# Flamingo block with two expert layers: plain scatters in layer 0, separate first groups, and weighted sums with the values as a 32-wide stationary operand

## The reference

```
x = x + tanh(g_xattn[0]) * attention0(layernorm(x), ctx)          # 16 heads of 16, biases, output projection
x = x + tanh(g_ffn[0])   * experts0(layernorm(x))                 # 8 experts, top 2, softmax gates, relu, F = 1024
x = x + tanh(g_xattn[1]) * attention1(layernorm(x), ctx, mask)    # 16 heads, causal, no output projection
x = x + tanh(g_ffn[1])   * experts1(layernorm(x))                 # 8 experts, sparsemixer top 2, silu(gate) * up, F = 512
```

## Time and profile before

| | |
|---|---|
| median of 3 runs | 1835.96 us (1834.67 to 1841.45) |
| the profiled execution | 1848.75 us, its span 1845.8 us |
| TensorE (PE) busy | 1653.4 us |
| VectorE (DVE), ScalarE (ACT), POOL busy | 1246.7, 1235.0, 876.2 us |
| share of the chain that ended last: TensorE, VectorE, ScalarE, DMA | 62%, 13%, 7%, 5% |

### The profile page before, as it was taken

One profiled execution on the slowest core, in us unless ns is written; L12 is line 12 of the kernel. 1 busy time (PEld: TensorE's weight loads), 2 busy tenths in 40 slices (PEclk: granted clock), 3 DMA queues, 4 the chain that ended last, 5 costly groups with the idle time before them and its releaser, 6 DMA issues.

```text
span 1845.8 us, 36500 instructions
## 1 busy us (share of the span) xinstructions
PE 1653.4 (90%) x12444; PEld 1559.8 (85%) x12444; DVE 1246.7 (68%) x2829; ACT 1235.0 (67%) x2873; POOL 876.2 (47%) x877
## 2 busy tenths in 40 slices
PE   3999989999499999999988599999999299999997
PEld 2898888888398988999988499989998299999997
DVE  2566656555578888898886456666666767676764
ACT  1666666656288877887876276666666177777775
POOL 2123332232456656676665311333332457777776
PEclk8999999999599999999999799999999599999999
DMA  2222221213567877888874322323322378888883
GB/s 94 47 58 75 66 67 47 75 53 92 147 185 211 220 204 204 219 223 211 213 201 129 91 53 63 85 83 87 87 58 81 117 205 232 232 232 230 228 232 108
DMA packets 215785, 255.90 MB, mean 139 GB/s; under 512 B 30768, under 2 KB 166192, under 8 KB 215472
## 3 DMA queue, kind: packets, MB, share of 16 engines
q1 hardware_dynamic: 185360, 218.26, 41.4%
q0 software_dynamic: 28608, 33.73, 9.3%
q10 hardware_dynamic: 1632, 1.59, 0.3%
HBM read 190.38 MB, written 49.97 MB: 130 GB/s over the span
## 4 chain that ended last, share of the span: by engine, by line
PE 62%; DVE 13%; ACT 7%; issue 6%; DMA 5%; POOL 2%; SPq 2%; another core or an unknown queue 2%; POOLq 0%; ACTq 0%; DVEq 0%
PE ps L372 13%; PE ps L374 13%; PE ps L373 13%; PE ps L490 11%; PE ps L392 5%; DVE KXR L1067 4%; DVE PTR L1096 3%; DMA U<-in_wpack 3%; DVE WR L1096 2%; ACT U L683 2%; PE ps L408 2%; PE ps L471 1%; ACT KXR L653 1%; POOL xs_scr L1175 1%
## 5 line engine op out<-in xcount | busy, mean ns | idle before, releaser
L1067 POOL TENSOR_TENSOR KXR<-U,KXR 128x1024 fp32r<-128x1024 f32 (+1 forms) x156 | 390.2, 2501 | 200.6 <-ACT KXR L653 200.6
L372 PE MATMUL ps<-QR,KXR 128*128 128x256 f32 x1248 | 363.4, 291 | 36.2 <-issue 23.2
L373 PE MATMUL ps<-QR,KXR 128*128 128x256 f32 x1248 | 356.1, 285 | 0.0
L374 PE MATMUL ps<-QR,KXR 128*128 128x256 f32 x1248 | 356.1, 285 | 0.0
L653 ACT ACTIVATE KXR<-U 128x1024 fp32r<-128x1024 f32 (+1 forms) x312 | 286.6, 945 | 78.3 <-DMA U<-in_wpack 55.7
L564 ACT ACTIVATE U<-ps,mx 128x128 f32<-128x128 f32 x1024 | 292.3, 381 | 13.0 <-DVE mx L927 7.5
L490 PE MATMUL ps<-VA,U 128*128 128x102 f32 x2048 | 271.1, 275 | 13.5 <-DVE U L937 9.5
L490 PEld LDWEIGHTS ps<-VA,U 128*128 128x128 f32 x2048 | 260.0, 194 | 25.3 <-DVE U L937 10.9
L372 PEld LDWEIGHTS ps<-QR,KXR 128*128 128x128 f32 x1248 | 240.0, 192 | 44.9 <-issue 29.3
L927 DVE TENSOR_REDUCE mx<-ps 128x4 f32<-128x512 f32 x256 | 175.4, 685 | 144.1 <-PE ps L408 62.0
L373 PEld LDWEIGHTS ps<-QR,KXR 128*128 128x128 f32 x1248 | 240.1, 192 | 0.0
(11 more groups left out here) (194 smaller groups left out, 4105.2 us busy)
## 6 DMA issues: line engine op xcount, KB each, us to landing
U<-in_wpack SPq DMA_DIRECT2D x234, 512.0 KB
U<-xs_scr SPq DMA_DIRECT2D x78, 258.0 KB
U<-in_wpack SPq DMA_DIRECT2D x78, 256.0 KB
KXR<-U SPq DMA_DIRECT2D x512, 32.0 KB
U<-in_ctx_t SPq DMA_DIRECT2D x16, 512.0 KB, 4.9
XR<-in_L_ffn_b SPq DMA_DIRECT2D x39, 128.0 KB
X<-in_x SPq DMA_DIRECT2D x8, 512.0 KB, 4.2
x_scr<-X SPq DMA_DIRECT2D x8, 512.0 KB
```

The costliest lines, as they stand in the source:

```text
L372: e.matmul(o, wh, xh, start=first, stop=False)
L373: e.matmul(o, wh, xl, start=False, stop=False)
L374: return e.matmul(o, wl, xh, start=False, stop=done)
L1067: e.tensor_tensor(w_cols(L, WL, n), w_raw(L, n), hi, ALU.subtract).then_inc(*l_w[n](L, i))
```

## The change

Three things are changed together.

Layer 0's experts write their rows, unscaled, to a place of their own for each of a token's two choices (`ys_scr`, 2 x 4096 rows), with a plain scatter. The gates stay in SBUF (`GT`), rows to the experts are one column shorter (`ROWS`), `act_y` is gone from layer 0, and so are the stores of `X`, which stays in SBUF. In layer 1 SP loads two rows per token (`sp_rows`) and VectorE adds both to `X`, multiplied by the gates (`dve_add_rows`).

The first group of each layer is written out apart (`pe_first`, `act_first`, `dve_first`, `sp_first`), `FIRST` is -8: keys and values come ahead of turns and queries, each constant is waited for where it is used, they are loaded in another order, four more banks are used, and in layer 0 twelve matmuls on a cleared tile go first (`WARM`). Layer 1's query, key and value weights and first contexts are loaded from tile 2 of layer 0's experts on (`sp_ahead`) and split at its end.

In the weighted sums the values of a head with the column of ones and what follows it (32 columns, `VA` is now flat) are the stationary operand, and the transposed probabilities move. The four heads of a step go to four groups of 32 partitions of `OB`. A batch's sums are copied out by ScalarE (`OS`), transposed by TensorE into a bank of `PTB`, which the probabilities' transposes share in turns (`pt_place`, `turn_free`), and then normalised; what follows comes one step later.

```diff
-                    for h in range(4):
-                        hh = 8 * m + 4 * z + h
-                        ins = e.matmul(OB[:, hh * 17:(hh + RV) * 17].rearrange("p (r d) -> p r d", r=RV), PT[:, i % 3, h],
-                                       VA[:, v, j % 2, hh:hh + 1, :].to_broadcast([128, RV, 17]), start=True, stop=True)
+                        w.wait_ge(*a_o[L, b - 1])
+                    for h in range(4):
+                        hh = 4 * (i % 4) + h
+                        ins = e.matmul(OB[32 * h:32 * h + 32, (i % 4) * 128:(i % 4) * 128 + 128], VA[:, v, j % 2, hh * 17:hh * 17 + 32],
+                                       PT[:, i % 3, h], start=True, stop=True)
...
+                if (b := bat(s, 6)) is not None:
+                    bank = pt_place["o", b]
+                    w.wait_ge(*a_o[L, b])
+                    turn_free(w, L, "o", b)
+                    for n in range(4):
+                        ins = e.transpose(bank[:, n * 128:(n + 1) * 128], OS[:, n * 128:(n + 1) * 128], ident)
+                    ins.then_inc(*m_o(L, b))
...
+                if (b := bat(s, 6)) is not None:
+                    w.wait_ge(*m_av[L, 4 * b + 3])
+                    if b:
+                        w.wait_ge(*m_o[L, b - 1])
+                    e.activation(OS[:, :], OB[:, :], ACT.Copy).then_inc(*a_o(L, b))
...
+        for n, (use, _, _) in enumerate(turns):
+            pt_place[use] = PTB[n % 2]
+            if n >= 2:
+                pt_before[use] = turns[n - 2][1:]
...
-                if (b := bat(s, 6)) is not None:
-                    w.wait_ge(*m_av[L, 4 * b + 3])
-                    o = OB[:, 0:272].rearrange("p (h d) -> p h d", d=17)
+                if (b := bat(s, 7)) is not None:
+                    w.wait_ge(*m_o[L, b])
+                    o = pt_place["o", b][:, :].rearrange("p (h d) -> p h d", d=32)
...
+        def pe_first(e, w, L):
+            if L == 0:
+                w.wait_ge(*s_kz[0, 0])
+                for n in range(WARM):
+                    e.matmul(PTB[1][:, :], KXR[:, 0:128], KXR[:, 0:512], start=True, stop=True)
+            for m in range(2):
+                pe_key(e, w, L, 0, m)
+            for h in range(2):
+                pe_value(e, w, L, 0, h)
+            for t in range(2):
+                pe_turn(e, w, L, 0, t)
+            for m in range(2):
+                w.wait_ge(*v_k[L, 0, m])
+                pe_query(e, w, L, 0, m)
...
+        def dve_add_rows(e, w, b):
+            w.wait_ge(*d_yl[b % 3][b])
+            e.scalar_tensor_tensor(X[:, b], YL[:, b % 3, 0], GT[:, 0, b:b + 1], X[:, b], ALU.mult, ALU.add).then_inc(*v_c.up())
+            w.wait_ge(*v_c.now)
+            e.scalar_tensor_tensor(X[:, b], YL[:, b % 3, 1], GT[:, 1, b:b + 1], X[:, b], ALU.mult, ALU.add).then_inc(*v_yl(b))
...
+                w.wait_ge(*v_h[0, NT - 1, 3])
+                sp_mask(e, w, 0)
                 experts_out(w, 0)
+                for b in range(3):
+                    sp_rows(e, w, b)
+                sp_keys(e, w, 1, 0)
+                sp_rows(e, w, 3)
+                sp_keys(e, w, 1, 1)
...
+        def sp_ahead(e):
+            for n, name in enumerate(("Wq", "Wk", "Wv")):
+                e.dma_start(WS[:, n], A["L1_xattn_" + name].rearrange("(t p) n -> p t n", p=128)).then_inc(*d_w2(n))
...
+                w.wait_ge(*m_y[L][L, i, a])
+                at = bass.IndirectOffsetOnAxis(ap=xi[:, i % 4, a:a + 1], axis=0)
+                if L == 0:
+                    ins = e.indirect_dma_start(ys_d[0], at, yo[:, r, a, :], None, bounds_check=2 * T - 1, oob_is_err=False)
+                else:
+                    ins = e.indirect_dma_start(ys_d[1], at, yo[:, r, a, :], None, bounds_check=T - 1, oob_is_err=False, compute_op=ALU.add)
```

More of the change, by code:

```diff
@@ L129, in grp @@
     g, m = divmod(s - k + 16, 16)
-    return g if m == 0 and 0 <= g < NG else None
+    return g if m == 0 and 0 < g < NG else None
 def bat(s, k):
@@ L346, in bank_free, with ct_low @@
                 w.wait_ge(*before[use])
+        def ct_low(L, g):
+            return (v_ct if (L, g) == (1, 0) else p_ct)[L, g]
         def banks_out(w, L):
@@ L520, in pe_down @@
             if i:
[L521 removed]
+                w.wait_ge(*m_y[L][L, i - 1, 1])
             for f in range(nf):
@@ new lines, in act_key @@
+        def act_key(e, w, L, g, m):
+            w.wait_ge(*m_k[L, g, m])
+            bank4 = place[L, "k", g, m][:, :].rearrange("p (b k) -> p b k", b=G)
+            if g >= 2 and m == 0:
+                for b in range((g - 1) * G - 2, (g - 1) * G):
+                    w.wait_ge(*d_k[b % 2][L, b, 7])
+            if L == 0:
+                w.wait_ge(*s_bq[0])
+                ins = e.activation(KT[:, g % 2, :, 0, m], bank4, ACT.Identity, bias=bqk[:, 1, m:m + 1])
+            else:
+                ins = e.activation(KT[:, g % 2, :, 0, m], bank4, ACT.Copy)
+            ins.then_inc(*a_k(L, g, m))
@@ L615, in act_attention @@
-                if L == 0 and (b := bat(s, 7)) is not None:
+                    act_context(e, w, L, g)
+                for at, take in ((X0, act_turn), (Q0, act_query), (K0, act_key), (V0, act_value)):
+                    for n in range(2):
+                        if (g := grp(s, at[n])) is not None:
+                            take(e, w, L, g, n)
+                if L == 0 and (b := bat(s, 8)) is not None:
                     w.wait_ge(*m_ot[b])
@@ new lines, in dve_key @@
+        def dve_key(e, w, L, g, m):
+            w.wait_ge(*a_k[L, g, m])
+            bank4 = place[L, "k", g, m][:, :].rearrange("p (b k) -> p b k", b=G)
+            hi, lo = KT[:, g % 2, :, 0, m].bitcast(F32), KT[:, g % 2, :, 1, m]
+            if L == 0:
+                ins = e.scalar_tensor_tensor(lo, bank4, bqk[:, 1, m:m + 1], hi, ALU.add, ALU.subtract)
+            else:
+                ins = e.tensor_tensor(lo, bank4, hi, ALU.subtract)
+            ins.then_inc(*v_k(L, g, m))
+        def dve_rests(e, w, L, s):
+            for at, rest in ((X0, dve_turn), (Q0, dve_query), (K0, dve_key)):
+                for n in range(2):
+                    if (g := grp(s, at[n])) is not None:
+                        rest(e, w, L, g, n)
+            if L == 0 and (b := bat(s, 8)) is not None:
@@ L1283, in sp_attention @@
+                if (b := bat(s, -8)) is not None and b >= 2:
+                    sp_keys(e, w, L, b)
                 if s == 121:
@@ L1305, in sp_experts @@
             for i in range(NT):
+                if L == 0 and i == 2:
+                    sp_ahead(e)
+                    for g in range(2):
+                        sp_context(e, w, 1, g)
                 if i + 2 < NT:
```

577 lines of the change are left out of this document (332 added, 245 removed).

## The result

The changed kernel takes 1758.3 us (median of 4 runs, 1754.96 to 1761.77), the kernel before 1836.45 beside it (1834.67 to 1841.45): a ratio of 0.957, with a 95% interval from 0.9542 to 0.9597. That is faster, by 78 us. The forecast was 1780 us with a range of 1720 to 1850. The profiled execution took 1754.96 us, its span 1753.2, against 1848.75 and 1845.8 before. So the two profiles lie 94 us apart, 16 more than the medians: the profiled execution of the kernel before was 12 us slower than its median.

What follows compares the result with a forecast made beforehand. TensorE was taken to bound attention, while something else held it up in layer 0's experts and at the starts. Terms -10 - 18 - 22 - 6 = -56 us gave 1793 profiled, 1780 on the median's basis; range 1720 to 1850.

Steps and rivals of the forecast that it cites:

- copy and transposes: Weighted sums: each batch adds a hidden ScalarE copy and four TensorE transposes, 0.36 us each batch, +23 us in all.
- the change of layers: Layer 1's start: weights fetched early, keys and values run while scatters land; first score earlier, -6 us (-12 to +3).
- the additions: Layer 1's attention: two more VectorE additions per batch, counted as hidden, 0 us (to +10).
- The likeliest case: Whole kernel: the eight sums' records partly overlap, held by instruction issue at 0.71 us a step; 1780 us, chance 0.42.
- The sums' matmuls: Attention's weighted sums: eight records a step fall from 0.87 to 0.71 us over 256 steps, -41 us (-72 to +18).
- I take 0.71, since nothing in the trace goes faster: Weighted sums: 16 instructions a step issue at 0.044 us each, as the transposes do, so a step takes 0.71 us.
- The five slots of the rival: Weighted sums: neighbouring heads overlap in program order, not held by issue; 0.59 us a step, -72 us, 1750 us; chance 0.27.
- the one given a chance of 0.04: Weighted sums: complete overlap of the heads in two slots, 0.24 us a step, -161 us, 1661 us; chance 0.04.
- the array empties: Weighted sums: each change of shape drains the array, 0.46 us more a step, 1.05 in all, +46 us, 1867; chance 0.18.
- the weighted sums together: Attention in both layers: matmuls -41, transposes +23, waits on the copy +5, later end of attention +3; -10 us in all.
- Plain scatters: Layer 0's experts: no scaling and shorter scatters on POOL free the next weights earlier; -18 us (0 to -35).
- First group of layer 0: Kernel start: keys and values come first, constants waited for where used; first score at 25.5 instead of 47.6, -22 us.

Runs made afterwards that it cites:

- a_oldsums: The changed kernel with the weighted sums of before (probabilities stationary, 102 value columns moving, no copy or transposes of sums): 1766.1 us, ratio 0.9757 to the kernel before.
- a_control2: The changed kernel unedited, run again in the third batch as the measure beside its edits: 1718.6 us, ratio 0.9495 to the kernel before.
- b_noscale: The kernel before without ScalarE's scaling by the gates in layer 0's experts, adding scatter kept: 1779.7 us, ratio 0.9846.
- b_plain: The kernel before with a plain scatter in layer 0, rows written over each other instead of added: 1777.9 us, ratio 0.9821.
- a_both: The changed kernel with layer 1's additions six steps earlier and the fourth batch's rows fetched ahead of the first key copies: 1712.7 us, ratio 0.9471.
- a_noadds: The changed kernel without layer 1's additions of expert rows except the first group's, rows still loaded: 1714.7 us, ratio 0.9471 to the kernel before.
- a_control: The changed kernel unedited, run in the second batch on a slower chip: 1762.7 us, ratio 0.9515 to the kernel before.

## Why the prediction came out as it did

The range held the time, and the sign was right; so were, nearly, the terms for copy and transposes, for the change of layers and for the additions. The likeliest case's account of the records was wrong. The 22 us between 1780 and 1758 look smaller than the errors in the terms: on the profiled executions, from which the terms were read, the forecast was 1793 and the time 1755.

**The sums' matmuls: forecast -41, by the rows -92 (256 x 0.36).** The step that failed is "I take 0.71, since nothing in the trace goes faster". The 16 instructions of a step start within 0.16 us, 0.010 each; the 0.044 read from the transposes was not the limit of the issue. The five slots of the rival were wrong too: 0.59 leaves no room for 0.36, and the records start in two rounds of four. Which head each belongs to, and so whether they leave the program's order, the trace does not tell. Two rivals were each half right. The overlap is complete, as in the one given a chance of 0.04: its two slots are 0.24 and measured 0.22. And a change of shape costs what stands between: 0.10 ahead, 0.05 behind and some 0.14 within, 0.29 a step against the 0.46 of "the array empties". By the rule that a change of tiling mode drains the engine (the Trainium skill, "TensorEngine Tiling (Array Packing)", Key Properties) the trace agrees that there is a price; whether it is a full drain no run here shows. Together 0.22 + 0.29 = 0.51, against the forecast 0.71. That the error stayed this small is luck: two things that the forecast held for rivals both happened, overlap worth (0.87 - 0.22) x 256 = 166 us and turns that cost 74.

**Of that gain a part came.** With +22 for the sums' transposes the rows make -70. a_oldsums against a_control2 shows what arrived, by their stages on chips that agree on the kernel before: layer 0's scores 375.9 to 344.3, layer 1's 374.3 to 347.0, -59; the two stretches behind the scores grew by 4.0 and 4.5, where +3 was forecast for both. In the median the ratios 0.9757 and 0.9495 differ by 0.026, 47 us, of which -10 had been forecast. So the weighted sums together, forecast -10, gave some -47 beside the other changes; this is the term that was furthest off. In the first comparison the attentions gave less, -28.5 and -4.2 with +2.0 behind them. There TensorE is idle for 23.8 us in layer 1's scores against 13.2 in a_control2; its waits in that stretch of the changed kernel show where:

```profile
PE ps L408 <- issue: 6.0, 8, 0.9
...
PE ps L469 <- issue: 2.2, 2, 1.7
```

The waits put down to "issue" are 10.0 us in all. The same kernel in a_control2 has none of them there; the last section has more on the chips.

**Copy and transposes: as forecast.** Four transposes of the sums take 0.35 to 0.36, 64 of them +23. The +5 for waits on the copy are hardly there: 1.0 us in layer 1's scores.

**Plain scatters: forecast -18 (0 to -35), measured -39.6, beyond the bound.** The mechanism stood: the plain scatter lasts 1115 ns on POOL instead of 1567, waits for nothing but the issue, and SP waits for the low half behind it for 58 us instead of 85 (560 to 900 us). Two sizes were off. TensorE's floor is 12.1 us a tile and not 11.7, and the tile reaches it, where I had left it 5% above and then taken half. b_noscale and b_plain show why half was wrong: either relief alone ends nearly all of TensorE's waits, so it was no matter of shares. The stage stands at TensorE's own time now, and nothing more is to be had there from POOL.

**First group of layer 0: forecast -22, measured -19.5 at the first score and -15.5 some steps on.** First score at 28.1 instead of 25.5. Two things were left out. The keys were counted at 0.235 a record: eight intervals at 0.43 instead add 8 x 0.19 = 1.5 us, over half of the 2.6. The twelve warming matmuls did not keep the clock up over the wait of 2.35 us; in a_control2 it fell within that wait, and all twelve key records came at 0.43. Whether they gave anything no run shows, for none leaves them out. And the forecast ended at the first score: the next group's context, now loaded behind the first group's inputs, holds up the fifth unit's scores by 3.5 us (5.2 to 5.4 in a_oldsums and a_control2), where the kernel before waits 0.7.

**Between the layers: forecast -6, measured -5.4.** The fourth batch's rows behind the key copies were the end of that chain, as the forecast said: a_both moves them, and 3.7 us more come off.

**Layer 1's additions: forecast 0 (to +10), measured 0 to +3.** a_noadds has 343.9 us of scores against 347.0, ratios 0.9471 against 0.9495 with intervals that overlap; in layer 0, where the two kernels do the same, their scores differ by 2.2. Beside the old sums they seem to cost more. Between b_plain and a_oldsums, both with the old sums, the scores grow by 5.5 us in layer 0 and 11.2 in layer 1. Of the 5.5, 4.5 are the wait ahead of the fifth unit's scores (5.2 us against 0.7). In layer 1 the largest part are waits of TensorE's sums for VectorE, which b_plain does not have; of a_oldsums:

```profile
PE ps L543 <- DVE U L1087: 6.8, 10, 0.9
```

L1087 is VectorE's product that normalises the sums of the batch before and frees their bank. With the new sums ScalarE's copy frees that bank, and of waits for the product only 2.3 us are left, in the transposes (a_control2). The forecast counted this at nothing, as mostly covered: so it was in b_plain, but not once the additions had come to VectorE. That the additions are the cause is argued and not shown: no run has the old sums without them.

## What to carry to other kernels

When a small stationary operand leaves most of TensorE's columns unused, put independent products in different groups of 32 output partitions: here their records overlapped fully. Then count the turns into and out of that shape, not the records: a turn cost 0.29 us here, more than the 0.22 of eight records, so gather all narrow work into as few turns as buffers allow. And when a stage has one engine ahead of all others, look for its floor first; here either of two reliefs gave nearly the whole distance, and the second added 0.1 to 0.3 us a tile. And when a start is brought forward, follow the chain some steps past the first result: the next load may be what is late.

## What the runs showed of the hardware

- Narrow products (128 rows, 32 columns, 128 moving f32 columns) take 0.11 us a record, and four groups of partitions run as fast as two. The 16 instructions of a step, loads and matmuls, start within 0.16 us.
- A turn from full-width matmuls into the 32-column form and back costs some 0.29 us in all: 0.10 ahead, behind transposes as behind scores, 0.14 within and at the end, 0.05 in the transposes behind.
- The same kernel took 1762.7 us on one chip and 1718.6 on another, and the kernel before 1851.5 and 1809.2: 44 and 42 us, with nearly the same ratio (0.9515 and 0.9495). The scores differ by 31.5 and 19.0 us (375.8 and 366.0 against 344.3 and 347.0), the stretches behind them by -3.7 and -2.8; the experts agree (473.1 and 472.4). On the slower chip TensorE's waits in layer 0's scores (30 to 340 us) name "issue", time in which it waited for nothing that the profile shows, and on the faster one they don't. a_control:

```profile
PE ps L408 <- issue: 9.2, 5, 4.0
```

  a_control2:

```profile
PE ps L408 <- ACT U L695: 6.0, 2, 5.4
```

  Those five waits are 9 of the 31 us of difference in that stage. The clock is about as much again: it falls in such waits or behind them, and stands at 0.50 in layer 0's scores for 27.3 us against 6.8; 20 us more at 0.43 a record instead of 0.235 lose some 9 (an estimate). The longest of the waits in a_control:

```profile
201.11 0.79 PE L408 MATMUL ps<-PTR,WR 128*128 128x512 f32 x1 [4.00 <-issue]
201.70 0.63 PE L409 MATMUL ps<-PTR,WR 128*128 128x512 f32 x1
202.12 0.63 PE L410 MATMUL ps<-PTR,WR 128*128 128x512 f32 x1
```

  The records behind it follow each other at 0.43. What the waits themselves come from the runs don't show.
- After 5.1 us of warming matmuls the granted clock was 1.00 through 2.35 us without work, and 0.50 from 0.5 us after the next matmuls began (12.3 to 15.7). In a_control2 it fell within a wait of 3.19 us. So a wait can cost clock in the work that follows it. Ahead of the trace's first entry of the clock (8.9 us) the pace of 0.43 for a 512-wide record shows the lower level, though a window there reads 1.00.
